# A convolution and whitening kernel on one core: the second sweep's prefetch in 64-partition quarters, one a unit, in place of 128-partition halves in every second unit

## The chip, the cores and the metric

The kernel runs on one core of a Trainium2 chip. The metric is the device time of one execution in microseconds (us); the median of several executions counts.

## What is computed

The input `x` is (4, 64, 256, 256) float32: four images of 64 channels. Layer 0 is a long convolution whose two-dimensional filter of each channel is an outer product of two one-dimensional filters of length 256, so it can be done as two triangular matrix products; layer 1 whitens over the channels. Cut to what matters:

```python
h = sin(freq * (z @ w1 + b1)); h = sin(freq * (h @ w2 + b2)); h = sin(freq * (h @ w3 + b3))
hx, hy = (h @ wo) * exp(-t * abs(deltas))            # one for X and one for Y
k = einsum('ijk,imk->ijmk', hx, hy)[0]               # per channel: outer product
y = irfft2(rfft2(x, s=(512, 512)) * rfft2(k, s=(512, 512)) / 512)[..., :256, :256]
x = y + x * bias[:, None, None]
# layer 1
x1 = transpose(x, (1, 0, 2, 3)).reshape(64, -1)
x1_s = x1[:, ::9]
mean1 = mean(x1_s, axis=-1, keepdims=True)
cov = x1_s @ x1_s.T / x1_s.shape[1] + 0.01 * eye(64)
out = isqrt_newton_schulz(cov, 5) @ (x1 - mean1)
```

## The kernel before

The work has three stages. **The convolution** is cut into 128 units (`UNITS`), one a channel and a pair of images: units 0 to 63 are the first sweep (images 0 and 1), units 64 to 127 the second (images 2 and 3). In every unit q TensorE (PE) makes `make_v(q+1)` and `make_y(q)`, 40 matmul instructions in all, from the four lines of `toeplitz` (L710 to L713); ACT rounds and flips (L446, L447, L456, L463, L465), DVE splits and finishes (`split_v` L552, `finish_y` L572, `split_t` L561, `sum_masked` L580), GpSimd splits x and masks y (L386, L421). The result y of a unit is stored to `convolved` in DRAM, since the whitening matrix is known only after all units. **The statistics** stage turns sampled sums into a 64x64 matrix. **The whitening** stage runs over 64 tiles of 1 MB: each is loaded from `convolved`, multiplied by the matrix on PE (L832), and stored to `out`.

Of the tiles of the first sweep, 14 (`KEPT`) are fetched from DRAM while the second sweep still computes, into a part of SBUF (`kept`, a region of `arena`) that the convolution does not use. These are the loads this case is about. They are issued by `load_kept`, in 28 pieces of 512 KB.

All DMAs of the convolution go out on one queue, that of SyncE (SP), in the order of this loop:

```python
for q in range(UNITS):
    if q > 0:
        load_x(q + 4)          # waits until y of unit q-1 is finished (y_done)
    store_y(q - 1)             # two stores of 64 partitions each
    ...
    load_hankel(q + 5)         # two loads of 128 KB: the filters of a later unit
    load_kept(q)
```

SP issues in this order and stands still when it waits. `finish_y(q)` on DVE waits until the two stores of unit q-2 have landed, since y has two buffers (`y_stored`). So a ring runs DVE `finish_y(q-2)`, SP `store_y(q-2)`, the DMA engines, DVE `finish_y(q)`. PE waits for DVE's `split_v` and `split_t`, which stand behind `finish_y` on DVE. The whitening waits for all pieces at once: `pe.wait_ge(kept_loaded, 16 * KEPT * PIECES)`.

Of the kernel before, what the change touches and what calls it, by code (L numbers as in the profile page):

```python
# [13 lines left out]
P = 128  # L14
B, C, S = 4, 64, 256
# [36 lines left out]
TW = TROWS * XW  # L52
SWEEP_TILES = ROWS // TROWS
TILES = SWEEPS * SWEEP_TILES
KEPT = 14
PIECES = 2


ARENA = 24 * TW
# [6 lines left out]
def conv_whiten(nc, x, first, hidden, columns, bias, out):  # L66
# [4 lines left out]
    with ExitStack() as ctx:  # L71
# [3 lines left out]
        def sem(name):  # L75
            return ctx.enter_context(nc.semaphore(name))
# [6 lines left out]
        def region(cols):  # L83
            taken[0] += cols
            return arena[:, taken[0] - cols:taken[0]]

        kept = region(KEPT * TW)
# [105 lines left out]
        kept_loaded = sem("kept_loaded")  # L193
# [54 lines left out]
        def _(sp):  # L248
# [4 lines left out]
            for k in range(2):  # L253
                h = slice(k * ORDER, (k + 1) * ORDER)
# [39 lines left out]
            def tile_in(t, lo, hi):  # L294
                sweep, rows = t // SWEEP_TILES, t % SWEEP_TILES
                return bass.AP(tensor=y_dram.tensor, offset=sweep * P * ROWS * XW + rows * TW + lo,
                               ap=[[ROWS * XW, P], [1, hi - lo]])

            def load_kept(q):
                n = (q - (C + 4)) // 2  # L300
                if q % 2 or not 0 <= n < KEPT * PIECES:
                    return
                w = TW // PIECES
                lo = n % PIECES * w

                for k in range(2):
                    sp.wait_ge(y_stored[k], 32 * (C // 2))
                sp.dma_start(kept[:, n * w:(n + 1) * w], tile_in(n // PIECES, lo, lo + w)).then_inc(kept_loaded, 16)

            for q in range(4):  # L310
                load_x(q)
# [11 lines left out]
            for q in range(UNITS):  # L323
                if q > 0:
                    load_x(q + 4)
                store_y(q - 1)
                if q == 0:
                    sp.wait_ge(filt_stored, 16 * 4)
                load_hankel(q + 5)
                load_kept(q)  # L330
# [351 lines left out]
        def _(pe):  # L682
# [135 lines left out]
            for t in range(TILES):  # L818
                if t < KEPT:
                    pe.wait_ge(kept_loaded, 16 * KEPT * PIECES)  # L820
                k = in_at[t]
# [44 lines left out]
```

## Time and profile before

| | |
|---|---|
| median of 3 runs | 927.05 us (924.65 to 927.64) |
| the profiled execution's own time | 924.7 us |
| span of its trace | 922.9 us |
| PE busy | 867.1 us, 94% |
| DVE busy | 572.5 us, 62% |
| GpSimd busy | 494.9 us, 54% |
| ACT busy | 401.2 us, 43% |
| DMA moved | 306.65 MB, mean 332 GB/s |

A time is in us from the start of the span. "DMA share" is the mean busy share of the 16 DMA engines, counted by the time that their packets took. A share near 1 does not say that no more bytes could pass: different stretches at that share moved bytes at different rates. A landing is the arrival of a DMA's last packet, counted from its issue. A row of waits gives the engine and line that waited, what released it, the total in us, how often, and the longest.

### The profile page before, as it was taken

Reading aid. Unit: us, or ns where it says so; the run is one execution under the profiler, and the core shown is the slowest. Engines: PE = TensorE matmul, PEld = TensorE weight load, DVE = VectorE, ACT = ScalarE, POOL = GpSimd, SP = SyncE. Lnnn points to the kernel's source line nnn. Section 1 sums busy time; section 2 is a strip of 40 time slices with the busy share of each in tenths; the row PEclk is TensorE's granted clock in tenths of the full one; section 3 lists DMA queues with packets and bytes.
Section 4 is the critical chain, followed back from the end, with each engine's and each line's share of the span. In section 5 each row is a group of like instructions: output and inputs, shape, how many; then the busy total and the mean of one; then the engine's idle time right before and its main releaser. Section 6 shows DMA issues by size and latency. Waiting matters only on the chain.

```text
span 922.9 us, 16153 instructions
## 1 busy us (share of the span) xinstructions
PE 867.1 (94%) x6252; PEld 728.6 (79%) x6252; DVE 572.5 (62%) x630; ACT 401.2 (43%) x718; POOL 494.9 (54%) x279
## 2 busy tenths in 40 slices
PE   8989999999999999999999999998999999877773
PEld 5989999999999999999999999998544444323221
DVE  3478888888888866777878787875333333322221
ACT  2455555555555535555555555551223333222220
POOL 1488888888888876777878787873000000000000
PEclk9989999999999999999999999999999999999997
DMA  4899999999999986999999999988999999999998
GB/s 134 262 288 285 287 284 287 286 284 287 286 283 286 287 279 203 332 348 334 347 326 347 344 331 350 351 294 272 406 394 428 426 426 425 428 427 426 427 427 366
DMA packets 99331, 306.65 MB, mean 332 GB/s; under 512 B 13302, under 2 KB 48311, under 8 KB 84663
## 3 DMA queue, kind: packets, MB, share of 16 engines
q1 hardware_dynamic: 99169, 305.49, 93.2%
q8 instruction: 50, 0.82, 0.3%
q14 instruction: 27, 0.21, 0.1%
q10 hardware_dynamic: 85, 0.12, 0.0%
HBM read 167.96 MB, written 137.61 MB: 331 GB/s over the span
## 4 chain that ended last, share of the span: by engine, by line
PE 82%; DMA 12%; issue 2%; DVE 1%; POOL 0%; ACT 0%; SPq 0%; DVEq 0%; POOLq 0%
PE ps L713 24%; PE ps L832 16%; PE ps L710 13%; PE ps L711 13%; PE ps L712 13%; DMA arena<-convolved 11%; PE ps L752 2%; PE ps L687 1%; DMA first_filters<-arena 1%; PE ps L772 0%; ACT arena L504 0%; POOL arena L421 0%; DVE arena L678 0%; DMA arena<-first_filters 0%; DVE arena L572 0%
## 5 line engine op out<-in xcount | busy, mean ns | idle before, releaser
L713 PE MATMUL ps<-arena 128*128 128x128 f32 x2048 | 394.5, 274 | 0.0
L710 PE MATMUL ps<-rounded 128*128 128x256 f32 x1024 | 374.1, 365 | 8.7 <-issue 5.8
L421 POOL TENSOR_TENSOR arena<-arena,mask 128x1024 f32<-128x1024 f32 x126 | 326.7, 2593 | 66.0 <-DVE arena L572 65.4
L713 PEld LDWEIGHTS ps<-arena 128*128 128x128 f32 x2048 | 315.1, 190 | 0.0
L711 PE MATMUL ps<-rounded 128*128 128x256 f32 x1024 | 288.2, 281 | 0.0
L712 PE MATMUL ps<-rounded 128*128 128x256 f32 x1024 | 288.0, 281 | 0.0
L832 PE MATMUL ps<-arena 128*128 128x512 f32 x488 | 216.0, 597 | 26.6 <-DMA arena<-convolved 26.6
L572 DVE SCALAR_TENSOR_TENSOR arena<-arena,bias_sb,ps 128x1024 f32<-128x1024 f32 x127 | 162.5, 1280 | 102.5 <-DMA convolved<-arena 61.5
L832 PEld LDWEIGHTS ps<-arena 128*128 128x128 f32 x488 | 90.7, 190 | 150.9 <-issue 105.0
L710 PEld LDWEIGHTS ps<-rounded 128*128 128x128 f32 x1024 | 197.4, 193 | 9.7 <-issue 9.7
L386 POOL TENSOR_TENSOR rounded<-arena,rounded 128x512 fp32r<-128x512 f32 x128 | 165.2, 1290 | 70.2 <-ACT rounded L456 69.7
L711 PEld LDWEIGHTS ps<-rounded 128*128 128x128 f32 x1024 | 197.6, 193 | 0.0
L712 PEld LDWEIGHTS ps<-rounded 128*128 128x128 f32 x1024 | 193.3, 189 | 0.0
L678 DVE TENSOR_SCALAR arena<-ps,small 128x1024 f32<-128x1024 f32 x64 | 82.2, 1284 | 171.6 <-PE ps L832 171.6
L580 DVE TENSOR_REDUCE arena<-arena 128x116 f32<-128x1044 f32 x126 | 155.5, 1234 | 0.0
L504 ACT ACTIVATE arena<-ps,small 128x1024 f32<-128x1024 f32 x64 | 71.3, 1115 | 189.7 <-PE ps L832 189.7
L463 ACT COPY arena<-ps 128x512 f32<-128x512 f32 x128 | 75.0, 586 | 156.2 <-PE ps L713 156.1
L456 ACT CAST rounded<-arena 128x512 fp32r<-128x512 f32 x128 | 80.3, 628 | 70.0 <-DMA arena<-x 68.1
L552 DVE TENSOR_TENSOR rounded<-ps,rounded 128x512 fp32r<-128x512 f32 x128 | 87.9, 687 | 29.0 <-ACT rounded L465 28.7
L561 DVE TENSOR_TENSOR rounded<-arena,rounded 128x512 fp32r<-128x512 f32 x127 | 89.7, 706 | 1.9 <-ACT rounded L447 1.9
L447 ACT CAST rounded<-arena 128x512 fp32r<-128x512 f32 x127 | 78.3, 616 | 0.0
L446 ACT COPY arena<-arena 128x256 f32<-128x256 f32 x127 | 51.3, 404 | 58.6 <-PE ps L713 58.3
(98 smaller groups left out, 217.7 us busy)
## 6 DMA issues: line engine op xcount, KB each, us to landing
arena<-x SPq DMA_DIRECT2D x128, 512.0 KB, 5.5
convolved<-arena SPq DMA_DIRECT2D x256, 256.0 KB, 5.3
out<-arena SPq DMA_DIRECT2D x64, 1024.0 KB, 13.5
arena<-convolved SPq DMA_DIRECT2D x47, 1024.0 KB, 19.0
arena<-filters SPq DMA_DIRECT2D x246, 128.0 KB, 4.7
arena<-convolved SPq DMA_DIRECT2D x28, 512.0 KB, 6.2
filters<-arena SPq DMA_DIRECT2D x4, 768.0 KB, 8.1
rounded<-convolved SPq DMA_DIRECT2D x3, 1024.0 KB, 10.7
```

What stands on the lines that cost most here:

```text
L386: nc.gpsimd.tensor_tensor(x_lo[k], row_block(q % X_SLOTS, 0), x_hi[k].bitcast(F32), ALU.subtract).then_inc(x_lo_done, 1)
L421: nc.gpsimd.tensor_tensor(masked_of(k, 0, PER), by_image(y_sb[k]), mask_of(q // C, 0, PER), ALU.mult).then_inc(masked_done, 1)
L552: nc.vector.tensor_tensor(v_lo[k], ps_v[k][:, :, 0:S], v_hi[k].bitcast(F32), ALU.subtract).then_inc(v_lo_done, 1)
L561: nc.vector.tensor_tensor(t_lo[k], hankel[h][:, :, ::-1], t_hi[k].bitcast(F32), ALU.subtract).then_inc(t_lo_done, 1)
L572: nc.vector.scalar_tensor_tensor(y_sb[k], x_sb[q % X_SLOTS], bias_sb[:, q % C:q % C + 1], ps_y[k].rearrange("p a n -> p (a n)"), ALU.mult, ...
L580: nc.vector.tensor_reduce(z_of(q % C), grouped(q % 2, 0, BLOCKS), AX_X, ALU.add).then_inc(z_done, 1)
L678: nc.vector.tensor_scalar(places[out_at[t]][:, TW // 2:TW], src, small[:, 6:7], None, ALU.add).then_inc(t_dve, 1)
L710: mm(wide, hi[:, b, cols], t_hi[k][:, f, :], start=True, stop=False)
L711: mm(wide, hi[:, b, cols], t_lo[k][:, f, :], start=False, stop=False)
L712: mm(wide, lo[:, b, cols], t_hi[k][:, f, :], start=False, stop=False)
L713: last = mm(o[:, b, m * S + P:(m + 1) * S], block1[:, b, cols], t_f32[k][:, f, :], start=False, stop=True)
L832: last = mm(ps[:, bank(t, u) + r, :], dmat, places[k][:, w:w + IMG], start=True, stop=True)
```

## The change

`PIECES` goes from 2 to 4. A tile of 128 partitions x 2048 columns came as two pieces of 128 partitions x 1024 columns (512 KB), one in each even unit from q = 68 to q = 122. It now comes as four pieces of 64 partitions x 1024 columns (256 KB), the lower 64 partitions and then the upper 64 of each half, one in every unit from q = 68 to q = 123. The bytes, the places, the total of the semaphore and the contiguous run of 4 KB in each partition stay as they are.

```diff
-PIECES = 2
+PIECES = 4
...
             def load_kept(q):
-                n = (q - (C + 4)) // 2
-                if q % 2 or not 0 <= n < KEPT * PIECES:
-                    return
-                w = TW // PIECES
-                lo = n % PIECES * w
+                n = q - (C + 4)
+                if not 0 <= n < KEPT * PIECES:
+                    return
+                w = TW // 2
+                t, lo, h = n // PIECES, n // 2 % 2 * w, n % 2 * (P // 2)
 
                 for k in range(2):
                     sp.wait_ge(y_stored[k], 32 * (C // 2))
-                sp.dma_start(kept[:, n * w:(n + 1) * w], tile_in(n // PIECES, lo, lo + w)).then_inc(kept_loaded, 16)
+                sp.dma_start(kept[h:h + P // 2, t * TW + lo:t * TW + lo + w], tile_in(t, lo, lo + w)[h:h + P // 2]
+                             ).then_inc(kept_loaded, 16)
```

On SP's queue a stretch of two units of the second sweep stands so before (`arena<-x` is `load_x`, `convolved<-arena` is `store_y`, `arena<-filters` is `load_hankel`, `arena<-convolved` is `load_kept`):

```order
L263 DMA arena<-x 128x1024
L292 DMA convolved<-arena 64x1024 x2
L282 DMA arena<-filters 128x1x256 x2
L308 DMA arena<-convolved 128x1024
L263 DMA arena<-x 128x1024
L292 DMA convolved<-arena 64x1024 x2
L282 DMA arena<-filters 128x1x256 x2
```

And the same stretch of the changed kernel, whose lines are numbered one higher:

```order
L264 DMA arena<-x 128x1024
L293 DMA convolved<-arena 64x1024 x2
L283 DMA arena<-filters 128x1x256 x2
L309 DMA arena<-convolved 64x1024
L264 DMA arena<-x 128x1024
L293 DMA convolved<-arena 64x1024 x2
L283 DMA arena<-filters 128x1x256 x2
L309 DMA arena<-convolved 64x1024
```

Each unit now has the same six DMAs, where five and six took turns; nothing moves on PE, DVE, ACT or GpSimd.

## Rows read from the trace of the kernel before

**Rows 1.** The page: shares of the chain that ended last.

```profile
PE 82%; DMA 12%; issue 2%; DVE 1%; POOL 0%; ACT 0%; SPq 0%; DVEq 0%; POOLq 0%
```

**Rows 2.** Windows (columns named): first sweep, second sweep, whitening.

```profile
core 0: us, PE busy (x) PEld busy (x) DVE busy (x) ACT busy (x) POOL busy (x), PEclk, DMA share, GB/s
115.00:276.00 161.00, 161.00 (x1398) 161.00 (x1397) 129.85 (x141) 87.75 (x175) 140.66 (x71) 1.00 0.92 286
368.00:621.00 253.00, 252.16 (x2180) 251.67 (x2179) 197.69 (x217) 138.34 (x273) 198.62 (x109) 1.00 1.00 339
690.00:805.00 115.00, 113.60 (x265) 49.80 (x263) 42.37 (x33) 36.79 (x33) 0.00 (x0) 1.00 1.01 427
```

**Rows 3.** Timeline of ACT, `round_v` (start, us): units 34 apart, then 58 apart.

```profile
118.90 0.59 ACT L463 COPY arena<-ps 128x512 f32<-128x512 f32 x1 [1.32 <-PE ps L713]
275.75 0.59 ACT L463 COPY arena<-ps 128x512 f32<-128x512 f32 x1 [1.32 <-PE ps L713]
...
356.75 0.59 ACT L463 COPY arena<-ps 128x512 f32<-128x512 f32 x1 [1.34 <-PE ps L713]
626.20 0.58 ACT L463 COPY arena<-ps 128x512 f32<-128x512 f32 x1 [3.54 <-PE ps L713]
```

**Rows 4.** Waits of PE between 368 and 621.

```profile
PE ps L710 <- issue: 0.8, 1, 0.8
```

**Rows 5.** Waits of DVE, first in 115 to 276, then in 368 to 621.

```profile
DVE arena L572 <- PE ps L713: 20.4, 33, 1.0
DVE arena L572 <- DMA convolved<-arena: 0.7, 1, 0.7
...
DVE arena L572 <- DMA convolved<-arena: 52.7, 35, 3.2
DVE arena L572 <- PE ps L713: 0.4, 1, 0.4
```

**Rows 6.** DMA issues with median landing: 115 to 276, then 368 to 621.

```profile
arena<-x SPq DMA_DIRECT2D x35, 512.0 KB, 5.1
convolved<-arena SPq DMA_DIRECT2D x70, 256.0 KB, 4.8
arena<-filters SPq DMA_DIRECT2D x70, 128.0 KB, 4.3
...
convolved<-arena SPq DMA_DIRECT2D x108, 256.0 KB, 6.0
arena<-convolved SPq DMA_DIRECT2D x27, 512.0 KB, 6.2
```

**Rows 7.** Timeline of SP's queue: one unit of each sweep.

```profile
210.27 0.33 SPq L263 DMA_DIRECT2D arena<-x  x1
210.65 1.11 SPq L292 DMA_DIRECT2D convolved<-arena  x2
211.85 2.02 SPq L282 DMA_DIRECT2D arena<-filters  x2
...
403.05 0.33 SPq L263 DMA_DIRECT2D arena<-x  x1
403.43 1.14 SPq L292 DMA_DIRECT2D convolved<-arena  x2
404.66 1.21 SPq L282 DMA_DIRECT2D arena<-filters  x2
405.97 0.67 SPq L308 DMA_DIRECT2D arena<-convolved  x1
408.03 0.33 SPq L263 DMA_DIRECT2D arena<-x  x1
```

**Rows 8.** Lines of SP's queue: issue in ns, min/median/max.

```profile
L292 SPq DMA_DIRECT2D convolved<-arena x256: 445/596/1531, 40.5 to 635.9; - x128
L282 SPq DMA_DIRECT2D arena<-filters x246: 526/878/1897, 38.6 to 609.7; - x123
L308 SPq DMA_DIRECT2D arena<-convolved x28: 533/542/874, 360.6 to 611.4; - x28
```

**Rows 9.** Waits of SP's queue between 368 and 621.

```profile
SPq L263 <- DVE arena L572: 23.4, 23, 2.0
```

## The prediction

> **What bounds the kernel now.** I read the chain that ended last, then the windows, then the waits of each engine in the second sweep. The chain is PE for 82% and DMA for 12% [rows 1]: the convolution is PE's and the whitening the DMA engines'. The windows show it: in both sweeps PE is busy all the time, in the whitening the DMA share is 1.01 at 427 GB/s [rows 2]. So a microsecond that PE loses in the second sweep moves everything behind it by the same amount, and the change can act only through PE's losses there. Bytes and the whitening stay as they are.
>
> How much does PE lose there? ACT's copy of v starts when PE releases it, which gives PE's pace: 156.85 us for 34 units in the first sweep is 4.613 us a unit; 269.45 us for 58 units of the second is 4.646 [rows 3]. At the first sweep's pace the 58 would take 267.6, so **1.9 us** are lost between units 69 and 127. One idle gap of 0.8 us is seen by itself [rows 4]; the rest is smaller.
>
> Why so little, with the DMA share at 1.00? Because a ring with slack stands between. In the first sweep `finish_y` on DVE waits for PE, 33 times, and for a store once; in the second it waits for stores 35 times, 52.7 us in all, and for PE once [rows 5]. The second sweep's DVE is thus paced by its own stores, landing in 6.0 us where it was 4.8 [rows 6], and PE lives on DVE being allowed to run late. The reader should see a ring near its limit: two units, 9.23 us, for `finish_y`, the issue, the landing.
>
> **The change, part by part.**
>
> *Bytes and transfer time.* A half is 524288 bytes: 1.23 us at the whitening's 427 GB/s, 1.55 us at the second sweep's 339 [rows 2]. A quarter is half of that, 0.61 to 0.77 us. A unit without a piece moves 1.31 MB, 3.07 us at 427 GB/s, so with a quarter 3.7 us of the unit's 4.61. Before, such a unit took turns between 3.07 and 4.3. Mean demand unchanged.
>
> *What the stores feel.* A kept piece is last in its unit, ahead of the next unit's x and y. Before, every second unit's store stood behind 1.2 to 1.5 us more than in the first sweep; now every one stands behind 0.6 to 0.8. In the ring: the first sweep's part is x issue 0.33, stores 1.11 [rows 7] and landing 4.8, near 6.2 us, with `finish_y` (1.3) 7.5 of 9.23 by medians. With a quarter ahead of each it is 8.1 to 8.3; with a half, 8.7 to 9.0 in one unit and 7.5 in the next. Landings scatter by more than a microsecond, which is why there are waits although the medians fit. Fewer rings over the limit means fewer late `split_t` and `split_v`, for which PE stalls. It can return at most the 1.9 us and at least nothing, if the stalls come from scatter that is there anyway. I take **1.2 us**: the gap of 0.8 that only an accumulated delay explains, and some of the rest.
>
> *SP's issues.* 28 more issues (56 for 28), each between 0.53 and 0.67 with its two waits already satisfied [rows 7, 8]: a 64-partition store takes 0.45 to 0.6, so a smaller piece is not cheaper. That is 15 us, 0.27 a unit on average, and 0.6 in those odd units that had none. What hides it: SP's own idling. In the first sweep SP ends a unit's issues at 213.87, 1.0 us before the next x, 214.9, one unit after 210.27 [rows 7]. In the second it waited for DVE in 23 of 53 units, 23.4 us [rows 9], so in the other 30 it was not ahead. The floor of a unit's issues is 0.33 + 1.11 + 1.20 + 0.55 and gaps of 0.3, 3.5 us; but the two filter loads take up to 2.0 instead of 1.2 [rows 7], with which it is 4.3, still under 4.61. Cost taken: 0, and 0.6 us a ring where SP is late. Behind the waiting or issuing SP stand load_x (four units early) and the next store, the one that counts.
>
> *Partitions.* A piece in 64 partitions uses half the width of a tile. Loads into 64 partitions do not occur in this stage; the nearest are the two 64-partition stores. In the first sweep x is issued at 210.27 and lands 5.1 later, at 215.4; the second filter load is issued near 212.9 and lands 4.3 later, at 217.2 [rows 6, 7]. In these 1.8 us both stores (0.5 MB) and the filters (0.25 MB) passed: about 430 GB/s, the full rate. At half rate the stores alone would need 2.4 us. So the row says no loss; but the two stores come in a pair that covers all partitions, and a quarter comes alone. From the row I take 0 more; the upper bound is a quarter at half of 427 GB/s, 1.23 us, so 0.6 us a unit more.
> The Trainium skill speaks against the change here: SBUF — State Buffer, section Door 1 (the DMA port swizzle), says that partitions 0 to 63 reach only 8 of the 16 DMA ports and run at half the rate. The stores' rate above does not agree with it, and no row shows a lone quarter; by it each quarter would take the 1.23 us of the upper bound.
>
> *End.* The last piece goes out one unit later, unit 123 for 122, four units ahead of the end; nothing waits for it until the whitening. Cost 0.
>
> **Sum.** The profiled execution took 924.7, its span 922.9. 924.7 - 1.2 + 0 + 0 = 923.5. The median of the runs before is 927.05, 2.35 over the profiled one, and no row says where those 2.35 went. Against the median: 927.05 - 1.2 = **925.8**.
>
> **The rivals.**
>
> 1. *The surplus is the same stalls.* If the 2.35 us by which ordinary runs exceed the profiled one are also PE stalls of the second sweep, and the even flow removes all: 927.05 - 1.9 - 2.35 = 922.8. For it: the stalls depend on chance scatter of landings, so runs should differ in them. Against: the ring stays within 1 us of its limit, so some stalls remain. Chance 0.19.
>
> 2. *A lone quarter runs at half rate.* Per unit 0.6 us more DMA time: 3.7 + 0.6 = 4.3 at best, 4.6 + 0.6 = 5.2 at the second sweep's own rate (1.573 MB at 339 GB/s is 4.64 a unit). It decides from 4.61 on. The bounds are 0 and 56 x 0.6 = 34 us; the middle of 4.3 and 5.2 is 4.75, 0.14 over, 56 x 0.14 = 8 us: 935. For: `finish_y` waits on stores already. Against: the stores' rate above. Chance 0.13.
> By the same section of the Trainium skill this rival is what happens, with 218 GB/s in place of 436 as its figures; the Trainium skill's DMA: Bandwidth & Descriptors, section Rules for kernel authors, adds that two transfers to disjoint partition halves serialize and should be one of 128. The trace has no lone half to set beside either.
>
> 3. *The ring goes over its limit in every unit.* Before, a delayed even unit was followed by a relieved odd one. Now each ring is 8.1 to 8.3 and, if SP is 0.6 late each time, 8.7 to 8.9 by medians, and with scatter over 9.23 in both parities; 0.2 over the limit is 0.1 a unit, 56 x 0.1 = 5.6 us: 932. For: SP was not ahead in 30 of 53 units. [...] Chance 0.11.
>
> 4. *It does nothing.* Stalls come from scatter alone, 927. Chance 0.12.
>
> **How the numbers follow.** The forecast, 925.8 with a range of its own of 924.3 to 927.5, has 0.45. A measurement of this kernel tells about 0.3%, 2.8 us, from no change. Faster by more: rival 1 and a little of the forecast's low end, 0.20. Slower by more: rivals 2 and 3, 0.24. Within: 0.56. The range leaves out some 0.08 below and 0.12 above: 922.5 to 933.
>
> **What the changed kernel's profile would show.** Right: ACT's L463 4.613 to 4.63 apart in the second sweep; `finish_y` waiting on stores much less than 52.7 us and again on PE; SP's waits at the x load below 23.4 us but present; quarters landing in under 6 us, each issued in 0.53 to 0.6; the DMA share 1.00 or less. Rival 2: quarters landing later than stores of the same size issued around them, x loads over 6.4 us late, PE gaps in many units. Rival 3: SP with no waits, `finish_y` waits in every unit at landings no longer than before. The prediction falls most easily by the 1.2 us, which no row gives, and by what a lone 64-partition load costs.

## The result: slower, by 3%

The changed kernel takes 953.6 us (median of 6 runs, 948.64 to 957.67) where the kernel before takes 927.19 (median of 6, 922.28 to 929.17). The ratio is 1.0295, with a 95% interval of 1.0259 to 1.0331: 26 to 27 us more. The profiled execution took 954.49 us, its span 952.7.

The page of the changed kernel, its chain of waits, by engine and by line:

```profile
PE 51%; DMA 34%; DVE 5%; SPq 5%; issue 2%; ACT 1%; POOL 0%; DVEq 0%; ACTq 0%; POOLq 0%
DMA convolved<-arena 23%; PE ps L834 15%; PE ps L715 12%; DMA arena<-convolved 11%; PE ps L712 7%; PE ps L713 7%; PE ps L714 7%; DVE arena L574 4%; SPq L293 2%; PE ps L754 1%; SPq L264 1%; SPq L283 1%; PE ps L689 1%; DMA first_filters<-arena 1%; PE ps L774 0%
```

PE had 82% of the chain [rows 1] and now has 51; 23% is now the stores of y (`convolved<-arena`), which were not in it. The ring of `finish_y`, the issue and the landing has become the bound of the second sweep. One turn of it stands in the chain so (start, us, what):

```profile
427.29 1.29 DVE arena L574
428.60 0.33 SPq L264
428.98 0.47 SPq L293
429.49 8.34 DMA convolved<-arena
437.85 1.29 DVE arena L574
```

From one `finish_y` of a buffer to the next it takes 10.56 us, which is over two units of PE (9.23), and 8.34 of it is the second store's way to its landing.

The second window of [rows 2], kept at its old ends:

```profile
368.00:621.00 253.00, 236.33 (x1963) 231.01 (x1962) 175.64 (x193) 119.16 (x245) 177.57 (x97) 0.99 1.04 302
```

The whitening is as before (share 1.01 at 427 GB/s in 720 to 835), and so is the first sweep (PE busy all the time, share 0.92 at 286 GB/s). In the second sweep the DMA share rose from 1.00 to 1.04 while the rate fell from 339 to 302 GB/s: the engines are busier and move less. That fits transfers that got slower, not transfers that start later.

ACT's copy of v, in the two units of [rows 3] between which 58 units lie:

```profile
356.85 0.58 ACT L465 COPY arena<-ps 128x512 f32<-128x512 f32 x1 [1.32 <-PE ps L715]
...
656.22 0.59 ACT L465 COPY arena<-ps 128x512 f32<-128x512 f32 x1 [3.54 <-PE ps L715]
```

299.37 us against 269.45, so 29.9 more, 5.16 us a unit in place of 4.65. The span grew by 29.8. The whole loss lies in these units. A small part of it, estimated at 1.5 us, is PE's clock: after its longest gap, 1.96 us that ended at 517.93, PE ran for 3.2 us at a granted clock of 0.50 (1.2 GHz in place of 2.4), and its `L712` matmuls started 1.06 us apart in place of 0.58 (window 519.2 to 522.4).

Waits between 368 and 621, of ACT, DVE and PE and then of SP's queue, and the landings of the same stretch:

```profile
ACT rounded L458 <- DMA arena<-x: 124.1, 48, 4.6
DVE arena L574 <- DMA convolved<-arena: 77.1, 49, 3.2
PE ps L712 <- issue: 16.2, 26, 2.0
```

```profile
SPq L264 <- DVE arena L574: 53.5, 42, 2.4
```

```profile
arena<-x SPq DMA_DIRECT2D x48, 512.0 KB, 7.8
convolved<-arena SPq DMA_DIRECT2D x96, 256.0 KB, 7.6
arena<-convolved SPq DMA_DIRECT2D x49, 256.0 KB, 8.0
```

DVE waits for stores in all 49 units, not in 35 of 53; stores land after 7.6 us where it was 6.0 [rows 5, 6]; a quarter needs 8.0, longer than a half of twice the bytes did (6.2). PE's one gap of 0.8 [rows 4] has become 26 gaps, 16.2 us. SP's queue has more time to spare than before (53.5 us against 23.4 in [rows 9]). So it is not SP that holds the ring here. ACT's wait for x is the longest in total, but it is not what ends last in the turn above: where x landed at 426.1, ACT had flipped the filters by 427.6, and `finish_y`, which `split_t` stands behind, ended at 428.6.

### The profile page after: what moved, and what is told of

Its sections match the earlier page's. It is cut to its first block, busy times and chain, and to the rows that moved or that the text cites. A ratio compares the mean times of both kernels' runs of the same rounds, so it can differ in the third digit from the quotient of the medians.

```text
span 952.7 us, 16209 instructions
## 1 busy us (share of the span) xinstructions
PE 878.9 (92%) x6252; PEld 734.6 (77%) x6252; DVE 571.0 (60%) x630; ACT 396.0 (42%) x718; POOL 495.4 (52%) x279
## 4 chain that ended last, share of the span: by engine, by line
PE 51%; DMA 34%; DVE 5%; SPq 5%; issue 2%; ACT 1%; POOL 0%; DVEq 0%; ACTq 0%; POOLq 0%
DMA convolved<-arena 23%; PE ps L834 15%; PE ps L715 12%; DMA arena<-convolved 11%; PE ps L712 7%; PE ps L713 7%; PE ps L714 7%; DVE arena L574 4%; SPq L293 2%; PE ps L754 1%; SPq L264 1%; SPq L283 1%; PE ps L689 1%; DMA first_filters<-arena 1%; PE ps L774 0%
## 5 line engine op out<-in xcount | busy, mean ns | idle before, releaser
L712 PE MATMUL ps<-rounded 128*128 128x256 f32 x1024 | 375.2, 366 | 26.8 <-issue 23.5
L712 PEld LDWEIGHTS ps<-rounded 128*128 128x128 f32 x1024 | 198.3, 194 | 33.9 <-issue 33.8
L467 ACT CAST rounded<-ps 128x512 fp32r<-128x512 f32 x128 | 75.6, 590 | 0.0
```

The costliest lines, as they stand in the source:

```text
L712: mm(wide, hi[:, b, cols], t_hi[k][:, f, :], start=True, stop=False)
```

## The experiments

Three causes were to be told apart: (1) a lone transfer to 64 neighbouring partitions runs at half rate, (2) the cadence with its sixth DMA in every unit, (3) 64-partition pieces in any arrangement. All ratios are to the kernel before, in runs on the same chip. The ratio is not exactly that of the two medians. `n` counts pieces; the lines shown replace the body of `load_kept`.

**A full-width quarter in every unit.**

```diff
-                w = TW // 2
-                t, lo, h = n // PIECES, n // 2 % 2 * w, n % 2 * (P // 2)
+                w = TW // PIECES
+                lo = n % PIECES * w
...
+                sp.dma_start(kept[:, n * w:(n + 1) * w], tile_in(n // PIECES, lo, lo + w)).then_inc(kept_loaded, 16)
```

> One piece in every unit as in the changed kernel, but 128 partitions x 512 columns (runs of 2 KB in place of 4 KB). Theory 1, a lone transfer to 64 neighbouring partitions runs at half rate: this one is spared, 925 to 930 us. Theory 2, the cadence is at fault (a piece and one more DMA on SP's queue in every unit puts the ring over its limit each time): slow as the changed kernel, 945 to 957 us. Theory 3, any 64-partition piece costs, alone or in a pair: 925 to 930, as theory 1.

Measured: 928.89 us against 928.52, ratio 1.0015 (0.9972 to 1.0058). Cadence and piece count stay, the 26 us are gone. Theory 2 falls as the cause of the loss; that the even flow would gain something falls as well. A small cost of the cadence is not excluded: the interval goes from -2.6 to +5.4 us, and in the trace DVE waits for stores in every unit (61.9 us, 53 times) and the 58 units take 276.15 us, 6.7 more than in the trace of before.

**Lower and upper quarters back to back in even units.**

```diff
+                m = (q - (C + 4)) // 2
+                if q % 2 or not 0 <= m < KEPT * 2:
+                    return
...
+                for h in (0, P // 2):
+                    sp.dma_start(kept[h:h + P // 2, t * TW + lo:t * TW + lo + w],
+                                 tile_in(t, lo, lo + w)[h:h + P // 2]).then_inc(kept_loaded, 16)
```

> Old cadence, every second unit, but each half comes as two 64-partition quarters back to back, lower and then upper; 56 issues as in the changed kernel. Theory 1: the two halves of the width overlap as the y stores do, 925 to 933 us. Theory 2: 927 to 930, the cadence being that of before. Theory 3, any 64-partition piece costs: 945 to 957 us.

Measured: 938.35, ratio 1.0115 (1.0040 to 1.0191). Between all the expectations: a pair is less bad than two lone quarters and still bad. It has 28 more issues than before as well, but in its trace SP waits 34.0 us for DVE, and the engines stand at a share of 1.03 with 317 GB/s, so the sign is that of width and not of SP.

**Every other partition.**

```diff
-                t, lo, h = n // PIECES, n // 2 % 2 * w, n % 2 * (P // 2)
+                t, lo, h = n // PIECES, n // 2 % 2 * w, n % 2
...
-                sp.dma_start(kept[h:h + P // 2, ...], tile_in(t, lo, lo + w)[h:h + P // 2]
+                sp.dma_start(kept[h:P:2, ...], tile_in(t, lo, lo + w)[h:P:2]
```

> The changed kernel with the same bytes, runs of 4 KB, 64 partitions a piece and one piece in every unit, but a piece takes every other partition (0, 2, 4, ... or 1, 3, 5, ...) in place of the lower or upper 64, in SBUF and in DRAM alike. Theory 1: 924 to 930 us. Theories 2 and 3 (cadence, count of rows, issues): unchanged, 948 to 957 us.

Measured: 936.48, ratio 1.0109 (1.0048 to 1.0171). Same bytes, same 64 rows, same issues, 17 us less than the changed kernel. Which partitions are taken is the larger part. But 8 us stay (10 by the ratio) that theory 1 does not explain, and their profile looks different. SP's queue, one unit and the next x:

```profile
453.35 0.57 SPq L264 DMA_DIRECT2D arena<-x  x1
453.97 1.11 SPq L293 DMA_DIRECT2D convolved<-arena  x2
455.18 2.22 SPq L283 DMA_DIRECT2D arena<-filters  x2
457.50 0.55 SPq L309 DMA_DIRECT2D arena<-convolved  x1
458.09 0.58 SPq L264 DMA_DIRECT2D arena<-x  x1
```

SP issues without a pause and needs 4.74 us for this unit, over PE's 4.61. Its waits for ACT and DVE between 368 and 621, and the chain between 450 and 470 by line:

```profile
SPq L283 <- ACT rounded L449: 10.8, 17, 0.9
SPq L264 <- DVE arena L574: 0.2, 1, 0.2
by line: DMA arena<-x 29.4%; SPq L283 27.4%; SPq L293 10.7%; issue 10.4%; SPq L309 10.0%; SPq L264 5.8%; ACT rounded L449 5.3%; ACT arena L448 4.0%; SPq L308 0.3%; SPq L209 0.2%; ACT rounded L458 0.1%; ACTq L209 0.1%
```

SP waited for DVE once in 50 units, so the ring is no longer held by the landing of the stores but by SP's issues. They are not alone in it: in 17 units SP also waits for ACT's flip of the filters, which waits for x, so the landing of x, issued late by SP, is part of the same ring.

**The rates by themselves.** The kernel before, with this at its end for lists of ten or twenty pieces (the last two are stores):

```diff
+            def phase(pieces):
+                s = ctx.enter_context(nc.semaphore(f"rate{len(rates)}"))
+                rates.append(s)
+                for at, t, lo, cols, rows in pieces:
+                    sp.dma_start(kept[rows, at:at + cols], tile_in(t, lo, lo + cols)[rows]).then_inc(s, 16)
+                sp.wait_ge(s, 16 * len(pieces))
```

> The kernel before with ten stretches of DMAs added at its end, each of some 5 MB and waited for: full-width loads; loads to the lower 64 partitions only; lower and upper in turn; every other partition in turn; even partitions only; full width with runs of 2 KB; full-width loads in turn with a lone lower or upper quarter; the same with a lone quarter of every other partition; stores from the lower 64 only; stores lower and upper in turn. Its time says nothing, its rates do. Theory 1: full width and every other partition near 400 GB/s, lower only near 210, and a lone quarter among full-width loads costs 0.3 to 0.6 us more than one of every other partition. Theories 2 and 3 without a port limit: all loads of 4 KB runs within 10% of each other.

Windows from the first packet of a list to its last; the last two numbers are DMA share and GB/s, and the 0.50 before them is the granted clock of TensorE, which is idle here. In this order: full width; lower 64 only; lower and upper in turn; every other partition, even and odd in turn; even only; full-width loads in turn with a lower or upper quarter; the same with an even or odd quarter; stores from the lower 64; stores lower and upper in turn.

```profile
927.69:942.66 14.97, 0.00 (x0) 0.00 (x0) 0.00 (x0) 0.00 (x0) 0.00 (x0) 0.50 0.92 350
944.34:969.93 25.59, 0.00 (x0) 0.00 (x0) 0.00 (x0) 0.00 (x0) 0.00 (x0) 0.50 1.01 205
972.12:994.26 22.14, 0.00 (x0) 0.00 (x0) 0.00 (x0) 0.00 (x0) 0.00 (x0) 0.50 1.01 237
996.20:1011.46 15.26, 0.00 (x0) 0.00 (x0) 0.00 (x0) 0.00 (x0) 0.00 (x0) 0.50 0.92 344
1013.07:1028.50 15.43, 0.00 (x0) 0.00 (x0) 0.00 (x0) 0.00 (x0) 0.00 (x0) 0.50 0.94 340
1047.96:1074.65 26.69, 0.00 (x0) 0.00 (x0) 0.00 (x0) 0.00 (x0) 0.00 (x0) 0.50 1.02 295
1076.46:1098.00 21.54, 0.00 (x0) 0.00 (x0) 0.00 (x0) 0.00 (x0) 0.00 (x0) 0.50 0.96 365
1099.58:1125.26 25.68, 0.00 (x0) 0.00 (x0) 0.00 (x0) 0.00 (x0) 0.00 (x0) 0.50 0.95 204
1126.72:1146.47 19.75, 0.00 (x0) 0.00 (x0) 0.00 (x0) 0.00 (x0) 0.00 (x0) 0.50 0.81 266
```

Another list, full width with runs of 2 KB, ran at 318. The lower 64 partitions are loaded at 205 GB/s, the even 64, spread over the width, at 340. In turn with full-width loads ten quarters cost 26.69 - 21.54 = 5.15 us more than ten even or odd ones, 0.5 us each. Lower and upper in turn do not repair it (237), in one queue; stores in pairs run at 266, not at the 430 that the prediction read into those of the kernel.

**SP's issues from ACT's queue**, for lower and upper quarters (first) and for every other partition (second). The load leaves SP's loop and stands at the end of ACT's unit:

```diff
                 round_x(q + 2)
                 flip(q + 2)
+                load_kept(q)
```

> The changed kernel with its lower and upper quarters issued from ACT's queue at the end of ACT's unit, in place of SP's. Two costs are held to be in the changed kernel's 26 us: some 17 for half-width pieces at half rate (it against every other partition), some 9 for SP's queue, which there never waited for DVE. If both are right: 940 to 948 us, the 9 gone and the 17 left. If SP's queue is not a cost of its own and the 9 are cadence or DMA load: 950 to 957. If half width is no cost by itself: 925 to 932.

> The kernel with every other partition in a piece, one in every unit, issued from ACT's queue in place of SP's. If the 8 to 9 us that it loses to the kernel before are SP's issues: 921 to 929 us, no slower than before. If they are the cadence or the DMA engines' load: 935 to 938, as from SP.

Measured: lower and upper 929.04, ratio 1.0025 (1.0008 to 1.0042); every other partition 923.78, ratio 0.9975 (0.9954 to 0.9995). The second is as expected: what was left of the loss goes when SP's queue is rid of the pieces. The first is not. It should have kept some 17 us and kept 2 or 3. Taken together with the changed kernel, moving a half-width piece from SP's queue to ACT's is worth 24 us. In the trace, that of the slowest execution of the ten (931.63), the 58 units take 276.03 us, 4.76 a unit. The edit also changes when in the unit a piece is issued, which was not tested apart in the kernel.

**A small sixth DMA in odd units.** The kernel before, and in its odd units 64 partitions x 32 bytes:

```diff
+                if q % 2 and 0 <= n < KEPT * PIECES:
...
+                    sp.dma_start(extra[0:P // 2], tile_in(n // PIECES, 0, 8)[0:P // 2]).then_inc(extra_loaded, 16)
+                    return
```

> The kernel before with one small load more in each odd unit of the second sweep, 64 partitions x 32 bytes into a buffer nobody reads, so that every unit issues six DMAs with the bytes of before. If the issues on SP's queue cost by themselves: 931 to 937 us. If an issue is hidden, as the prediction had it, and bytes or width make the loss: 925 to 930.

Measured: 936.60, ratio 1.0111 (1.0079 to 1.0143). 28 issues that move 57 KB in all cost 10 us. So a sixth issue on SP's queue need not be hidden. But its price is not a fixed one: the full-width quarters add the same 28 issues and cost -2.6 to +5.4 us, an interval that does not touch this one (7 to 13).

**The unit's mix by itself.** The kernel before with four lists of loads and six of units at its end; a unit is an x load, two stores, two filter loads and pieces as named, all from SP without a wait.

> The kernel before with stretches of DMAs added at its end. Four are loads of 5 MB in 64-partition pieces: lower partitions from neighbouring rows of DRAM; lower partitions from every other row; every other partition from neighbouring rows; every other partition from every other row. If the SBUF side sets the rate, the first two run near 205 GB/s and the last two near 340; if the DRAM side, the first and third near 205. Then six stretches of ten units' DMAs without any wait between them (x, two stores of y, two filter loads), with no piece, a half in every second unit, a lower or upper quarter in each, a quarter of every other partition in each, a 128 x 512 quarter in each, and a lower and an upper quarter in every second. A unit of PE is 4.61 us. By the half-rate theory a unit takes 0.3 to 0.6 us more with lower or upper quarters than with those of every other partition, and only the former is over 4.61; if SP's issues bound the strided one too, it is over 4.61 with SP's queue never idle and the DMA engines partly idle.

First the four lists of loads, from first packet to last (SBUF side / DRAM side): lower / neighbouring rows; lower / every other row; every other / neighbouring; every other / every other.

```profile
921.63:947.51 25.88, 0.00 (x0) 0.00 (x0) 0.00 (x0) 0.00 (x0) 0.00 (x0) 0.50 1.01 203
949.53:975.41 25.88, 0.00 (x0) 0.00 (x0) 0.00 (x0) 0.00 (x0) 0.00 (x0) 0.50 1.01 202
977.37:992.76 15.39, 0.00 (x0) 0.00 (x0) 0.00 (x0) 0.00 (x0) 0.00 (x0) 0.50 0.93 341
994.39:1010.08 15.69, 0.00 (x0) 0.00 (x0) 0.00 (x0) 0.00 (x0) 0.00 (x0) 0.50 0.92 335
```

The SBUF side alone sets the rate. Then ten units each, from the first issue to the last packet, so with the start and the last landings in it (the first list takes 43.8 us, though SP passes a unit in 4.05): no piece; a half every second unit; lower or upper in each; even or odd in each; 128 x 512 in each; lower and upper every second.

```profile
1010.47:1054.30 43.83, 0.00 (x0) 0.00 (x0) 0.00 (x0) 0.00 (x0) 0.00 (x0) 0.50 0.92 299
1054.58:1100.12 45.54, 0.00 (x0) 0.00 (x0) 0.00 (x0) 0.00 (x0) 0.00 (x0) 0.50 0.98 345
1100.55:1154.09 53.54, 0.00 (x0) 0.00 (x0) 0.00 (x0) 0.00 (x0) 0.00 (x0) 0.50 0.99 294
1154.91:1207.29 52.38, 0.00 (x0) 0.00 (x0) 0.00 (x0) 0.00 (x0) 0.00 (x0) 0.50 0.93 300
1207.80:1259.09 51.29, 0.00 (x0) 0.00 (x0) 0.00 (x0) 0.00 (x0) 0.00 (x0) 0.50 0.93 307
1259.47:1311.10 51.63, 0.00 (x0) 0.00 (x0) 0.00 (x0) 0.00 (x0) 0.00 (x0) 0.50 0.97 305
```

Only the first two are under ten of PE's units (46.1 us). The other four are over it by more than start and end explain, and the price of half width hides in them: 53.5 against 52.4, because the list of every other partition is held by SP (share 0.93) and that of lower and upper by the engines (0.99). SP's queue in the first and the third list, each without any wait:

```profile
1014.09 0.60 SPq L387 DMA_DIRECT2D arena<-x  x1
...
1015.88 2.21 SPq L395 DMA_DIRECT2D arena<-filters  x2
1018.14 0.59 SPq L387 DMA_DIRECT2D arena<-x  x1
...
1111.21 2.26 SPq L395 DMA_DIRECT2D arena<-filters  x2
...
1120.58 1.28 SPq L395 DMA_DIRECT2D arena<-filters  x2
```

A unit of five issues takes SP 4.05 us even with nothing to wait for (1014.09 to 1018.14). The two filter issues take 2.0 to 2.9 us in every unit of the first list, whose engines keep up (share 0.92), and mostly fall to 1.2 or 1.3 in the course of the second and the third, which SP leaves 10 and 11 us before their last packet.

**The same bytes and issues as before, half the width.** 28 pieces in the even units, 64 partitions x 2048 columns, so with runs of 8 KB:

```diff
-                w = TW // PIECES
-                lo = n % PIECES * w
+                t, h = n // PIECES, n % PIECES * (P // 2)
...
-                sp.dma_start(kept[:, n * w:(n + 1) * w], tile_in(n // PIECES, lo, lo + w)).then_inc(kept_loaded, 16)
+                sp.dma_start(kept[h:h + P // 2, t * TW:(t + 1) * TW], tile_in(t, 0, TW)[h:h + P // 2]
+                             ).then_inc(kept_loaded, 16)
```

> The kernel before with pieces of the same 512 KB, in the same every second unit and with the same 28 issues, but shaped 64 partitions x 2048 columns (runs of 8 KB), lower and then upper. Nothing is added to SP's queue, so only the width is tested. If half width runs at half rate and this counts from SP's queue: a piece takes 2.5 us in place of 1.2 to 1.5, 0.5 to 0.6 us a unit, and the unit in the mix with pieces on two sides is over 4.61: 935 to 955. If the changed kernel's loss needs the additional issues: 925 to 930.

Measured: 951.93, ratio 1.0281 (1.0216 to 1.0345). This is the loss of the changed kernel, with neither its additional issues nor its cadence; the 58 units take 299.78 us here and 299.37 there. Its window:

```profile
368.00:621.00 253.00, 230.69 (x1947) 226.63 (x1946) 176.99 (x195) 119.48 (x243) 177.74 (x98) 1.00 1.03 304
```

Again a share over 1 at 304 GB/s.

**Halves of the kernel before from ACT's queue.** The edit is that of the quarters from ACT, with the 28 halves of 128 partitions.

> The kernel before with its 28 halves, 128 partitions in every second unit, issued from ACT's queue in place of SP's. If the kernel before loses its 1.9 us and its scatter to the issues on SP's queue: as every other partition from ACT, 921 to 925 us, 0.2 to 0.4% faster than before. If the even flow of quarters made that gain: no different from before, 925 to 928.

Measured: 922.41, ratio 0.9953 (0.9929 to 0.9977). Faster than both kernels, by 2 to 7 us against the one before. Waits of DVE and of SP's queue, 368 to 621:

```profile
DVE arena L577 <- PE ps L718: 28.1, 46, 0.6
DVE arena L577 <- DMA convolved<-arena: 7.7, 9, 1.2
```

```profile
SPq L264 <- DVE arena L577: 40.2, 51, 1.5
```

DVE waits for PE again, as in the first sweep [rows 5], and SP is ahead in nearly every unit. The traces don't show the whole gain: the 58 units take 269.12 us against 269.45, but the trace of before is of one of its faster executions (924.7), and none of its slower ones was profiled.

**The mix on two queues.** The units' five DMAs from SP, ten pieces from ACT beside them, all ten issued in the first 7 us:

```diff
+            for k, pieces in enumerate([[(low, 1024), (high, 1024)], [(even, 1024), (odd, 1024)], [(full, 512)],
+                                        [(low, 1024)]]):
+                act.wait_ge(started, 16 * (k + 1))
+                for n in range(10):
+                    at, (rows, cols) = n * 2560 + 1536, pieces[n % len(pieces)]
+                    act.dma_start(kept[rows, at:at + cols], tile_in(n, 0, cols)[rows]).then_inc(other_done, 16)
```

> The kernel before with five stretches at its end, each of ten units' DMAs (x, two stores, two filter loads) on SP's queue without waits, and beside them on ACT's queue ten pieces: lower and upper quarters in turn; every other partition in turn; 128 x 512; lower quarters only; none. On SP's queue alone the lower and upper quarters took 54.4 us, every other partition 52.9, 128 x 512 51.7, none 44.1. If a half-width piece hurts because all that follows stands behind it in one queue: lower and upper near the others here, 46 to 49 us. If it costs the same port time from any queue: 52 to 54 for lower and upper, 46 to 48 for the other shapes.

Lower and upper; even and odd; 128 x 512; none (a list with lower pieces only took 48.4):

```profile
927.33:975.94 48.61, 0.00 (x0) 0.00 (x0) 0.00 (x0) 0.00 (x0) 0.00 (x0) 0.50 1.00 324
978.11:1021.92 43.81, 0.00 (x0) 0.00 (x0) 0.00 (x0) 0.00 (x0) 0.00 (x0) 0.50 0.99 359
1024.07:1068.12 44.05, 0.00 (x0) 0.00 (x0) 0.00 (x0) 0.00 (x0) 0.00 (x0) 0.50 0.99 357
1121.12:1165.53 44.41, 0.00 (x0) 0.00 (x0) 0.00 (x0) 0.00 (x0) 0.00 (x0) 0.50 0.89 295
```

Here half width costs 48.6 - 43.8 = 4.8 us for ten pieces, 0.5 each, as among the lone loads. With the other shapes ten pieces cost nothing: the last list, without pieces, leaves the engines a share of 0.89 and the others 0.99. Neither expectation was met in full: the lower and upper pieces are not near the others, and they are 5 us under their time in one queue.

## Why the prediction was wrong

**The step that failed: "From the row I take 0 more".** The prediction weighed half width and took no cost, because in the first sweep two stores and two filter loads seemed to pass in 1.8 us. That number is a difference of median landings, and a landing is the arrival of a DMA's last packet, while nothing says when its first one went; it is no duration of the stores. By themselves paired stores of that size run at 266 GB/s and not at 430, and lower ones alone at 204. The loads are at 203 to 205. The Trainium skill, SBUF — State Buffer, section Door 1, had said so: 64 neighbouring partitions reach half of the ports. The trace agrees now, with 205 against 350 GB/s, and with 340 once the same number of partitions is spread over the whole width. The run with half-width pieces of 512 KB (1.0281) shows that half width on SP's queue is enough for the changed kernel's loss, without its cadence and its issues. From ACT's queue the changed kernel's quarters lose 2 or 3 us, so it takes the queue too.

**Rival 2 was the case, mis-sized.** It was given 0.13 and 8 us, with 34 as its bound. Measured are 29.9 us in the second sweep, and its signs are there: x lands after 7.8 us, PE has gaps in many units, and a quarter lands after 8.0 where a store of its size takes 7.6. Its working had two ends, 4.3 us a unit if the engines reach 427 GB/s and 5.2 at the second sweep's own rate; the changed kernel has 5.16. The middle was no better founded than the ends: the mix of 1 KB and 4 KB packets with two stores of half width had never run at 427, and the row of the same stretch (339) should have counted. In the mix by itself ten units before the change take 45.5 us, start and end included, and with lower or upper quarters 53.5, 0.8 a unit more; PE's ten are 46.1. There was no room for 0.5.

**SP's issues at 0: wrong too, though not what decided.** The small sixth DMA cost 10 us, the quarters of every other partition 8 to 10. The floor of 3.5 us a unit took the short filter issues (1.2). They are short where the DMA engines are behind and long (2.0 to 2.9) where they keep up, and there SP needs 4.05 us with five issues; with the sixth the unit shown took 4.74, over 4.61. This is rival 3, with the signs that it named: in the run with every other partition SP has next to no wait for DVE, `finish_y` waits for stores 51 times, and the stores land no later than before (5.7 us against 6.0). In the changed kernel half width binds and SP waits 53.5 us; the two do not add there, since the pieces of 512 KB lose as much without the issues (1.0281 and 1.0295). Nor are the loads of x out of the way, which the prediction took as four units early: ACT waits for x 48 times between 368 and 621 in the changed kernel, though something else ends last there, and the landing of x is 29% of the chain between 450 and 470 with every other partition.

**The gain of 1.2 us by an even flow: not there.** Full-width quarters in every unit gain nothing (1.0015). The kernel before does have a remedy, another queue for its halves, uneven as they are: 0.9953. Quarters of every other partition from there, one in each unit, are no better (0.9975). Rival 1 had held the 2.35 us between the median and the profiled execution for stalls of the same kind; that 3.9 us of the median go with SP's queue fits it, but no slow execution was profiled, so it is not shown. What part of the gain from ACT's queue is SP's time and what part the shorter queue ahead of the stores was not separated.

**What was right:** the loss could come only through PE's second sweep and passes to the end one to one (29.9 us there, 29.8 in the span); DVE's wait for stores is the place where it enters, and the ring adds up as the prediction added it: 1.3 + 0.33 + 1.11 and the landing of 7.6 are 10.3 us, as are two units of 5.16; the last piece's later unit costs nothing.

**Open.** Why half-width pieces cost the kernel 26 us from SP's queue and 2 or 3 from ACT's. The mix shows the same without the kernel around it: with two queues ten units of lower and upper pieces take 53.5 - 48.6 = 4.9 us less. SP's own issues do not explain that, since the DMA engines are at a share of 1.03 from 10 us on in the one-queue list:

```profile
1110.00:1120.00 10.00, 0.00 (x0) 0.00 (x0) 0.00 (x0) 0.00 (x0) 0.00 (x0) 0.50 1.03 290
```

Between 1076 and 1086, in the list with halves, the same share moved 378 GB/s. Nor is it the moment of issue alone, since in the two-queue list the pieces are all issued at its start and in the kernel one a unit. That half-width packets hold up what stands behind them in their own queue, and less what stands in another, is a possible reading; no run shows it. Also open: why the same 28 more issues on SP cost next to nothing as 128 x 512 quarters, 8 to 10 us as every other partition and 10 as a DMA of 2 KB, though SP's queue is nearly full in the first two (51.3 and 52.4 in the mix).

## What to carry to other kernels

Cut a transfer along its columns, not along its partitions: loads to 64 neighbouring partitions ran at 205 GB/s where those over the whole width ran at 350. If it must be 64, every other partition keeps the rate (340). Where the order on one issuing queue sets the pace, count its issues by a stretch in which it never waits, and move independent prefetches to another engine's queue; here that gave 0.5%, and the even flow from SP none.

## What the runs showed that was not expected

- Two filter issues on SP take 2.26 us early in a list of DMAs and 1.28 later in the same list, when the engines are behind (1111.21 and 1120.58 above). So SP's busy time in a loaded stretch understates what it needs in an unloaded one.
- 28 more DMAs of 2 KB on a nearly full queue cost the kernel 10 us; 28 more of 256 KB, spread over the whole width in every other partition, cost 8 to 10. Few bytes do not make an issue cheap.
- Lower and upper in turn from one queue reach 237 GB/s for loads and 266 for stores, a little over one side alone (205, 204) and far from 350.
- Ten pieces of 128 x 512 or of every other partition, issued from ACT beside a full SP queue, cost no time at all (44.05 and 43.81 against 44.41 us without them), so the 2.6 MB passed in what SP's issues had left idle.
